# Dummy products on TensorE: 13 instead of 8 at the start of a fused decoder layer, and none near its end

## The chip, the cores and the metric

The kernel runs on one core of one Trainium2 chip. The metric is device time in microseconds (us) of the whole program; the kernel before was timed three times.

## The reference

One decoder layer over 16 sequences of 256 rows of 128 numbers, in three stages, each followed by a residual and a layer norm. The middle stage attends from 256 rows to 64 context rows with 16 heads of 64. The last stage is a gated network whose inputs and weights are rounded in blocks of 16 to the eight magnitudes of FP4.

```python
x = _layernorm(x + _L0_attn_ref(x, Wq, bq, Wk, bk, Wv, bv, Wo, bo, gamma, beta))   # linear attention, 16 heads of 8
x = _layernorm(x + _L0_xattn_ref(x, ctx_1024, Wq, Wk, Wv, Wo))                     # softmax over 64 context rows
x = _layernorm(x + _L0_ffn_ref(x, w_gate, w_up, w_down))
# the last stage:
gate, y = fp4_linear(x, w_gate), fp4_linear(x, w_up)      # 128 -> 352
h = silu(gate) * y
return fp4_linear(h, w_down)                              # 352 -> 128
```

## The kernel before

All weights and the context stay on chip. A sequence is two tiles (t = 0, 1) of 128 rows. The work is written as small steps, one function per step and engine (`gate_up`, `h_transpose`, `down` and so on on TensorE), and every engine has its own list of calls, written out by hand, in which the steps of several sequences b are interleaved. Nothing reorders them at run time: an engine takes its list in order, and each step waits on semaphores for its inputs and for the buffer that it overwrites. So the place of a call in the list sets what can stand behind a wait.

The run has three parts. First comes the set-up, named the fold in the change's description: the cross attention's query and key weights are multiplied into `GT` (`g_product`, written `F<-wqkT` and `TP<-wqkT`), and `GT` with the context into `M` (`m_product`, `F<-ctx_r,GT` and so on, 32 of them, each of three passes over high and low halves of the operands). `project_kv(0)` (`A<-kv_bias_r,ones_r` and `A<-w_attn,xT`) stands between the two `g_product`s. The steady part follows. In the end the last sequence goes tile by tile, with functions whose names begin with `tile_`.

Three calls of `keep_warm` put products on TensorE whose results nobody reads. The first multiplies zeros (`A<-fold`, since the zeros lie in a `fold` buffer) WARM times at the very start. The other two multiply the identity matrix into bank TP0 (`TP<-ident`): 7 times ahead of `h_transpose(13)` and 14 times ahead of `h_transpose(14)`. `h_transpose(b)` transposes `hv`, the rounded activations, which GpSimd finishes at L441 (POOL in the profile); ScalarE (ACT) copies the result to `hT` (L1089), and `down(b)` (L2895) multiplies it with the down weights. In the last sequence `tile_h_transpose` (L2922) and `tile_down` (L2928) do the same for one tile. VectorE (DVE) adds the residual after it (L1915, or L2003 by tile).

An fp32 product shows as two records of the trace in most rows: 8 products of 128x128 are "x16". A transpose of 128x128 is one record.

`xf_r`, two buffers, holds the high and low halves of the transposed inputs of the last stage for sequences 0 to 14; `xfT` is the same in full for the last sequence.

Of the kernel before, what the change touches and what calls it, by code (L numbers as in the profile page):

```python
# [7 lines left out]
FP32R = mybir.dt.float32r  # L8
# [5 lines left out]
P = 128  # L14
# [3 lines left out]
def decoder_layer(nc, x, x_t, attn_w, attn_rows, ctx_t, wq_t, wk_t, wv_t, wo_in, fw_in, out):  # L18
# [40 lines left out]
    with es:  # L59
        def sb(name, shape, dt=FP32):  # L60
            return es.enter_context(nc.sbuf_tensor(name, shape, dt))
# [83 lines left out]
        ssum = several("ssum", 2, [P, HX])  # L145
        srec = several("srec", 2, [P, HX])
# [95 lines left out]
        normed = {"attn": yan_made, "post": x1_made, "cross": x2_made, "ffn": out_made}  # L242

        XO_OF, GU_OF = (A2, A1), ((F0, F1), (S0, S1))

        def part(w, t):
            return w[:, t * P:t * P + P]
# [19 lines left out]
        def wait_free(eng, s, done):  # L267

            if done > 0:
                eng.wait_ge(s, done)  # L270
# [94 lines left out]
        def _(pool):  # L365
# [54 lines left out]
            def fold_halves(b, t):  # L420
                n = T * b + t
                pool.wait_ge(pe_made, n + 1)
                wait_free(pool, ssum_made, n - 1)
                p4 = pe_[n % NPE][:, :].rearrange("p (h s r) -> p h s r", h=HX, s=2)
                ge.tensor_tensor(by_head(fold[n % 2][:, :]), p4[:, :, 0, :], p4[:, :, 1, :], ALU.add).then_inc(fold_made, 1)  # L425

            def probabilities(b, t):
                n = T * b + t
                pool.wait_ge(srec_made, n + 1)
                w = by_head(pe_[n % NPE][:, :])  # L430
                ge.tensor_tensor(w, w, spread(srec[n % 2][:, :], HX, R), ALU.mult).then_inc(pn_made, 1)  # L431

            def x_dequantise(b):
                pool.wait_ge(xg_made, b + 1)
# [507 lines left out]
        def _(act):  # L942
# [101 lines left out]

            def cross_norm(b, t):
                wait_free(act, yf_made, b - 2)
                norm("cross", b, t, x2[b % 3][:, NBX * t:NBX * t + NBX, 0:BLK], blocks(yx[b % 2][:, t, :], NBX))

            def ffn_norm(b, t):
                norm("ffn", b, t, yf[b % 2][:, t, :], yf[b % 2][:, t, :])  # L1050

            def keep_x1T(b):
                act.wait_ge(x1T_made, b + 1)
# [19 lines left out]
                sc.activation(xc, xv[b % 2][:, :], ACT.Abs, scale=STEP).then_inc(xc_made, 1)  # L1073

            def keep_xfT(b):
                act.wait_ge(xf_cut_made, b + 1)
                sc.activation(xf_r[b % 2][:, 0, :], xf_cut[:, :], ACT.Copy).then_inc(xfT_kept, 1)

            def gate_tanh(b, t):
                act.wait_ge(gu_made, T * b + t + 1)  # L1080
# [18 lines left out]
                tile_norm("cross", b, t, x2[b % 3][:, NBX * t:NBX * t + NBX, 0:BLK], blocks(yx[b % 2][:, t, :], NBX))  # L1099

            def tile_ffn_norm(b, t):
                tile_norm("ffn", b, t, yf[b % 2][:, t, :], yf[b % 2][:, t, :])

            def tile_x2_magnitudes(b, t):
                act.wait_ge(xv_made, b + t + 1)
# [1 line left out]

            def tile_keep_xfT(b, t):
                act.wait_ge(xfT_made, b + t + 1)
                sc.activation(part(xfT, t), part(A2, t), ACT.Copy).then_inc(xfT_kept, 1)  # L1110

            def tile_gate_tanh(b, t):
                act.wait_ge(gu_made, T * b + t + 1)
# [558 lines left out]
        def _(dve):  # L1672
# [128 lines left out]
            def statistics(n, b):  # L1801
                y, made = {"attn": (x1[b % NA], ya_made), "post": (x1[b % NA], za_made), "cross": (yx[b % 2], yx_made),
                           "ffn": (yf[b % 2], yf_made)}[n]
                dve.wait_ge(made, b + 1)
# [21 lines left out]
            def score_sums(b, t):  # L1826
                n = T * b + t
                dve.wait_ge(fold_made, n + 1)
                ve.tensor_reduce(ssum[n % 2][:, :], by_head(fold[n % 2][:, :]), AX.X, ALU.add).then_inc(ssum_made, 1)  # L1829

            def score_reciprocals(b, t):
                n = T * b + t
                dve.wait_ge(ssum_made, n + 1)
                wait_free(dve, pn_made, n - 1)
                ve.reciprocal(srec[n % 2][:, :], ssum[n % 2][:, :]).then_inc(srec_made, 1)  # L1835

            def cross_residual(b):
                dve.wait_ge(o_made, T * b + T)
# [85 lines left out]
                ve.tensor_tensor(yx[b % 2][:, t, :], XO_OF[t][:, 0:P], x1[b % NA][:, t, :], ALU.add).then_inc(yx_made, 1)  # L1924

            def tile_statistics(n, b, t):
                y, made = {"cross": (yx[b % 2], yx_made), "ffn": (yf[b % 2], yf_made)}[n]
                dve.wait_ge(made, b + t + 1)
                wait_free(dve, mv_made[n], b)
                ve.bn_stats(stats[n][:, t, :], y[:, t, :]).then_inc(stats_made[n], 1)  # L1930

            def tile_aggregate(n, b, t):
                dve.wait_ge(stats_made[n], b + t + 1)
# [66 lines left out]
            def tile_ffn_residual(b, t):  # L2000
                dve.wait_ge(dn_made, b + t + 1)
                wait_free(dve, out_stored[b % 2], 16 * (b // 2))
                ve.tensor_tensor(blocks(yf[b % 2][:, t, :], NBX), blocks(part(A2, t), NBX), x2[b % 3][:, NBX * t:NBX * t + NBX, 0:BLK],  # L2003
                                 ALU.add).then_inc(yf_made, 1)

            biases()
# [725 lines left out]
        def _(pe):  # L2732
# [121 lines left out]
            def cross_out(b, t):  # L2854
                n = T * b + t
                pe.wait_ge(pT_kept, n + 1)
                if t == 0:
                    pe.wait_ge(vo_kept, b + 1)
                for j in range(NJ):
                    last = te.matmul(A2[:, t * P:t * P + P], pT[n % 2][:, j, :], vo[b % 2][:, j, :], start=(j == 0),  # L2860
                                     stop=(j == NJ - 1))
                last.then_inc(o_made, 1)

            def xf_transpose(b):
# [5 lines left out]
            def gate_up(b, t):  # L2870
                if b == 0 and t == 0:
                    pe.wait_ge(fwT_kept, 4)
                    pe.wait_ge(gu_high_made, 2)
                    pe.wait_ge(gu_low_made, 2)
                pe.wait_ge(xfT_kept, b + 1)
                pe.wait_ge(xf_low_made, b + 1)
# [14 lines left out]
            def down(b):  # L2891
                pe.wait_ge(hT_kept, b + 1)
                for t in range(T):
                    for k in range(NK):
                        last = te.matmul(DN[:, t * P:t * P + P], hT[b % 2][:, t, k * P:k * P + P], w_dn[:, k, :],  # L2895
                                         start=(k == 0), stop=(k == NK - 1))
                last.then_inc(dn_made, 1)

            def tile_cross_out(b, t):
# [12 lines left out]
            def tile_gate_up(b, t):  # L2912
                pe.wait_ge(xfT_kept, b + t + 1)
                for m, bk in enumerate(GU_OF[t]):
                    last = te.matmul(bk[:, 0:I], part(xfT, t), w_gu[:, m, :], start=True, stop=True)
                last.then_inc(gu_made, 1)

            def tile_h_transpose(b, t):
# [5 lines left out]

            def tile_down(b, t):
                pe.wait_ge(hT_kept, b + t + 1)
                for k in range(NK):
                    last = te.matmul(part(A2, t), hT[b % 2][:, t, k * P:k * P + P], w_dn[:, k, :], start=(k == 0), stop=(k == NK - 1))  # L2928
                last.then_inc(dn_made, 1)

            def keep_warm(bank, n, w=ident[:, :]):
# [709 lines left out]
```

## Time and profile before

| | |
|---|---|
| median of 3 runs | 374.0 us (372.37, 374.0, 375.88) |
| profiled execution, its own time | 374.35 us |
| its span, first to last instruction | 372.6 us |
| TensorE busy | 351.0 us, 94% of the span |
| VectorE busy | 307.9 us, 83% |
| GpSimd, ScalarE busy | 269.1 us (72%), 253.4 us (68%) |
| mean granted TensorE clock | 0.996 |

The span is one execution as the hardware profiler saw it; 1.75 us of its own time lie outside of the span. Busy shares are means over parts with different limits, so the parts are read by themselves. The granted clock is 1.0 at 2.4 GHz and 0.5 at 1.2 GHz. PE is TensorE, and DVE, ACT and POOL are the engines named above.

### The profile page before, as it was taken

The numbers are of one execution on the slowest core, as the hardware profiler recorded it, in microseconds if no ns is written. First come the engines' busy times: TensorE is split into PE (matmuls) and PEld (weight loads), VectorE is DVE, ScalarE is ACT, GpSimd is POOL, SyncE is SP. The second block draws the span as 40 slices with busy tenths as digits, with TensorE's granted clock in tenths as the row PEclk, the third lists the DMA queues.
The fourth block names the chain that finished last, engine by engine and source line by source line (L and its number), as shares of the span: only waits on it lengthen the run. The fifth ranks groups of instructions, "written<-read, shape, count | busy, mean of one in ns | idle before, by whom it ended". The sixth has DMA issues, their size and how long they took to land.

```text
span 372.6 us, 7321 instructions
## 1 busy us (share of the span) xinstructions
PE 351.0 (94%) x2143; PEld 268.7 (72%) x2143; DVE 307.9 (83%) x858; ACT 253.4 (68%) x533; POOL 269.1 (72%) x453
## 2 busy tenths in 40 slices
PE   7999998999998999999999999999999999998874
PEld 6688655775775968778678867786777788887663
DVE  2798756658689998869989779979998998999994
ACT  2757867586677678668687767868767656864553
POOL 4403549967988689969779895898989569784535
PEclk9999999999999999999999999999999999999998
DMA  7900100001000001000000000000000000000010
GB/s 251 300 2 16 30 1 14 16 16 29 15 17 14 2 15 43 16 30 17 15 29 14 17 1 17 28 3 0 17 15 2 15 2 0 8 23 14 3 30 28
DMA packets 13586, 10.44 MB, mean 28 GB/s; under 512 B 971, under 2 KB 12396, under 8 KB 13548
## 3 DMA queue, kind: packets, MB, share of 16 engines
q1 hardware_dynamic: 12540, 7.89, 7.0%
q10 hardware_dynamic: 1008, 2.10, 1.7%
q8 instruction: 18, 0.29, 0.3%
q14 instruction: 20, 0.16, 0.1%
HBM read 7.88 MB, written 2.10 MB: 27 GB/s over the span
## 4 chain that ended last, share of the span: by engine, by line
PE 71%; POOL 8%; DVE 8%; issue 6%; ACT 5%; DMA 1%; POOLq 0%; ACTq 0%; DVEq 0%
PE A L2860 13%; PE S L2833 12%; PE TP L2823 7%; PE F L2879 6%; PE TP L2851 6%; PE A L2895 5%; PE A L2784 3%; PE S L2842 3%; PE TP L2762 2%; POOL pe L431 2%; PE S L2762 2%; PE F L2762 2%; PE TP L2888 2%; PE A L2797 2%; DMA wqkT<-in_wk_t 1%
## 5 line engine op out<-in xcount | busy, mean ns | idle before, releaser
L431 POOL TENSOR_TENSOR pe<-pe,srec 128x1024 f32<-128x1024 f32 x32 | 60.9, 1904 | 9.2 <-DVE srec L1835 8.9
L2833 PE MATMUL S<-M,x1T 128*128 128x512 f32 x128 | 60.7, 597 | 1.5 <-ACT pe L1064 1.4
L2860 PEld LDWEIGHTS A<-wvoT,wqkT 128*128 128x128 f32 x480 | 56.4, 192 | 3.1 <-issue 1.8
L2860 PE MATMUL A<-wvoT,wqkT 128*128 128x128 f32 x480 | 58.0, 276 | 0.1
L425 POOL TENSOR_TENSOR fold<-pe 128x512 f32<-128x512 f32 x32 | 40.8, 1276 | 14.5 <-ACT pe L1064 14.2
L1818 DVE TENSOR_REDUCE smax<-S 128x16 fp32r<-128x1024 f32 x32 | 38.7, 1210 | 3.2 <-PE S L2833 3.1
L1064 ACT ACTIVATE pe<-S 128x1024 f32<-128x1024 f32 x32 | 32.6, 1020 | 10.6 <-PE S L2842 10.3
L1069 ACT ACTIVATE wqkT<-TP 128x1024 f32<-128x1024 f32 x32 | 32.6, 1019 | 4.3 <-PE TP L2851 4.1
L2833 PEld LDWEIGHTS S<-M,x1T 128*128 128x128 f32 x128 | 22.2, 190 | 18.3 <-issue 15.3
L2879 PE MATMUL F<-w_gu_r,xf_r 128*128 128x352 f32 x168 | 35.0, 344 | 0.1
L2851 PE MATMUL TP<-ident,pe 128*128 128x128 f32 x256 | 33.5, 274 | 1.6 <-POOL pe L431 1.0
L2851 PEld LDWEIGHTS TP<-ident,pe 128*128 128x128 f32 x256 | 28.8, 140 | 6.2 <-issue 3.1
L2823 PE MATMUL TP<-HW,ctx_f 128*64 128x512 f32 x128 | 31.0, 605 | 0.0
L2879 PEld LDWEIGHTS F<-w_gu_r,xf_r 128*128 128x128 f32 x168 | 26.9, 188 | 4.4 <-issue 3.2
L2895 PEld LDWEIGHTS A<-w_dn,hT 128*128 128x128 f32 x180 | 21.5, 192 | 6.6 <-issue 4.7
L441 POOL TENSOR_TENSOR hv<-hv,ham 128x704 f32<-128x704 f32 x15 | 20.8, 1389 | 6.0 <-DVE hv L1910 5.8
L1829 DVE TENSOR_REDUCE ssum<-fold 128x16 f32<-128x512 f32 x32 | 21.7, 677 | 4.2 <-POOL fold L425 4.2
L416 POOL TENSOR_TENSOR kn<-fk,ky 128x256 f32<-128x256 f32 x16 | 10.1, 632 | 20.7 <-DVE ky L1790 20.6
L2895 PE MATMUL A<-w_dn,hT 128*128 128x128 f32 x180 | 23.0, 277 | 2.0 <-ACT hT L1089 2.0
L2842 PE MATMUL S<-smax,ident_r 128*128 128x512 f32 x64 | 21.8, 422 | 1.7 <-DVE smax L1818 1.7
L409 POOL TENSOR_TENSOR xb<-x_sb,rows 128x512 f32<-128x512 f32 x16 | 20.4, 1275 | 3.9 <-DMA rows<-in_attn_rows 2.7
L1058 ACT ACTIVATE wvoT<-TP 128x1024 f32<-128x1024 f32 x16 | 16.3, 1022 | 6.8 <-PE TP L2823 6.8
(247 smaller groups left out, 890.2 us busy)
## 6 DMA issues: line engine op xcount, KB each, us to landing
xT<-in_x_t SPq DMA_DIRECT2D x16, 128.0 KB, 2.1
x_sb<-in_x SPq DMA_DIRECT2D x16, 128.0 KB, 2.1
out<-yf SPq DMA_DIRECT2D x15, 128.0 KB, 1.8
M<-in_fw SPq DMA_DIRECT2D x1, 560.0 KB, 11.0
wqkT<-in_wq_t ACTq DMA_DIRECT2D x2, 256.0 KB, 4.5
wqkT<-in_wk_t ACTq DMA_DIRECT2D x2, 256.0 KB, 5.8
ctx_f<-in_ctx_t ACTq DMA_DIRECT2D x2, 256.0 KB, 6.9
wvoT<-in_wv_t ACTq DMA_DIRECT2D x1, 512.0 KB, 9.2
```

The lines of the kernel that those rows point to most:

```text
L425: ge.tensor_tensor(by_head(fold[n % 2][:, :]), p4[:, :, 0, :], p4[:, :, 1, :], ALU.add).then_inc(fold_made, 1)
L431: ge.tensor_tensor(w, w, spread(srec[n % 2][:, :], HX, R), ALU.mult).then_inc(pn_made, 1)
L1064: sc.activation(pe_[n % NPE][:, :], S[:, :], ACT.Exp, scale=SCALE).then_inc(pe_made, 1)
L1069: sc.activation(pT[n % 2], TP[:, :].rearrange("p (a n) -> p a n", a=NJ), ACT.Copy).then_inc(pT_kept, 1)
L1818: ve.tensor_reduce(smax[n % 2][:, :], by_head(S[:, :]), AX.X, ALU.max, negate=True).then_inc(smax_made, 1)
L2823: last = te.matmul(TP[par * R:par * R + R, half * BANK:half * BANK + BANK], ctx_f[:, b * R:b * R + R], HW[:, par, 4 * half:4 * half + 4, : ...
L2833: last = te.matmul(S[:, half * BANK:half * BANK + BANK], x1T[b % 2][:, t * P:t * P + P], M[:, b // BH, HC * half:HC * half + HC, b % BH * ...
L2842: last = te.matmul(S[:, half * BANK:half * BANK + BANK], ident_r[:, :], spread(smax[n % 2][:, HC * half:HC * half + HC], HC, R), start=Fal ...
L2851: last = te.transpose(TP[:, j * P:j * P + P], pe_[n % NPE][:, j * P:j * P + P], ident[:, :])
L2860: last = te.matmul(A2[:, t * P:t * P + P], pT[n % 2][:, j, :], vo[b % 2][:, j, :], start=(j == 0), stop=(j == NJ - 1))
L2879: last = te.matmul(bk[:, 0:I], part(xf_r[b % 2][:, left, :], t), w_gu_r[:, right, m, :], start=(n == 0), stop=(n == len(PARTS) - 1))
L2895: last = te.matmul(DN[:, t * P:t * P + P], hT[b % 2][:, t, k * P:k * P + P], w_dn[:, k, :], start=(k == 0), stop=(k == NK - 1))
```

## The change

WARM goes from 8 to 13. Both later calls of `keep_warm` are taken out. `xf_r` is no longer memory of its own: its two buffers become slices of `GT`, which holds the folded weights at the start. `xfT` becomes two buffers, taken in turn by the sequence's number; only the last sequence uses it. The number of `fold`, `ssum` and `srec` buffers gets the name NFO with its old value 2. The diff also brings branches for `WHOLE_GATE`, `SUM_ON_PE` and `TILE_SUM_ON_PE`, which are empty or False, so none of their code is generated; the `down` functions show the pattern.

```diff
-        NXB, NA, NPE = 4, 5, 3
+        NXB, NA, NPE, NFO = 4, 5, 3, 2
...
-        fold = several("fold", 2, [P, HX * R // 2])
+        fold = several("fold", NFO, [P, HX * R // 2])
...
-        xf_r = several("xf_r", 2, [P, 2, T * P], FP32R)
-        xfT = sb("xfT", [P, T * P])
+        xf_r = [GT[:, k, 0:2 * T, :].rearrange("p (s t) n -> p s (t n)", s=2) for k in range(2)]
+        xfT = several("xfT", 2, [P, T * P])
...
+        WHOLE_GATE = ()
+        SUM_ON_PE = ()
+        TILE_SUM_ON_PE = False
...
-        WARM = 8
+        WARM = 13
...
             def tile_down(b, t):
                 pe.wait_ge(hT_kept, b + t + 1)
+                if TILE_SUM_ON_PE:
+                    pe.wait_ge(x2_made, T * b + t + 1)
+                    te.matmul(blocks(part(DN_OF[t], t), NBX), ident[:, :], x2[b % 3][:, NBX * t:NBX * t + NBX, 0:BLK],
+                              start=True, stop=False)
...
             pe.wait_ge(hT_kept, 13)
-            keep_warm(TP0, 7)
             h_transpose(13)
...
             pe.wait_ge(hT_kept, 14)
-            keep_warm(TP0, 14)
             h_transpose(14)
```

On TensorE, at the start of the program: the dummy products of zeros, then `g_product(0)`, `project_kv(0)` and `g_product(1)`. Before:

```order
L2934 MATMUL A<-fold 128x128 x8
L2742 MATMUL F<-wqkT 128x128 x8
L2782 MATMUL A<-kv_bias_r,ones_r 128x256
L2784 MATMUL A<-w_attn,xT 128x256
L2782 MATMUL A<-kv_bias_r,ones_r 128x256
L2784 MATMUL A<-w_attn,xT 128x256
L2742 MATMUL TP<-wqkT 128x128 x8
```

The changed kernel, at the same place (its line numbers are higher throughout, since the file grew):

```order
L2980 MATMUL A<-fold 128x128 x13
L2771 MATMUL F<-wqkT 128x128 x8
L2811 MATMUL A<-kv_bias_r,ones_r 128x256
L2813 MATMUL A<-w_attn,xT 128x256
L2811 MATMUL A<-kv_bias_r,ones_r 128x256
L2813 MATMUL A<-w_attn,xT 128x256
L2771 MATMUL TP<-wqkT 128x128 x8
```

Five more products stand ahead of the first `g_product`; nothing else moved. On TensorE, near the end of the program, from `gate_up(14, 1)` to the last `tile_down`. Before:

```order
L2879 MATMUL F<-w_gu_r,xf_r 128x352 x6
L2934 MATMUL TP<-ident 128x128 x7
L2888 MATMUL TP<-ident,hv 128x128 x6
L2910 MATMUL A<-ident,xv 128x128
L2915 MATMUL F<-w_gu,xfT 128x352 x2
L2895 MATMUL A<-w_dn,hT 128x128 x6
L2910 MATMUL A<-ident,xv 128x128
L2915 MATMUL S<-w_gu,xfT 128x352 x2
L2934 MATMUL TP<-ident 128x128 x14
L2888 MATMUL TP<-ident,hv 128x128 x6
L2895 MATMUL A<-w_dn,hT 128x128 x6
L2922 MATMUL TP<-ident,hv 128x128 x6
```

The changed kernel at the same place:

```order
L2916 MATMUL F<-w_gu_r,GT 128x352 x6
L2925 MATMUL TP<-ident,hv 128x128 x6
L2951 MATMUL A<-ident,xv 128x128
L2956 MATMUL F<-w_gu,xfT 128x352 x2
L2936 MATMUL A<-w_dn,hT 128x128 x6
L2951 MATMUL A<-ident,xv 128x128
L2956 MATMUL S<-w_gu,xfT 128x352 x2
L2925 MATMUL TP<-ident,hv 128x128 x6
L2936 MATMUL A<-w_dn,hT 128x128 x6
L2963 MATMUL TP<-ident,hv 128x128 x6
```

The two rows of `TP<-ident` are gone, and `gate_up` reads its inputs from slices of `GT`. The lists of the other engines hold the same operations and waits in the same order.

## Rows read from the trace of the kernel before

**Rows 1.** The page: TensorE's busy time, and its granted clock in 40 slices

```profile
PE 351.0 (94%) x2143; PEld 268.7 (72%) x2143; DVE 307.9 (83%) x858; ACT 253.4 (68%) x533; POOL 269.1 (72%) x453
...
PEclk9999999999999999999999999999999999999998
```

**Rows 2.** The page: the chain that ended last, by engine

```profile
PE 71%; POOL 8%; DVE 8%; issue 6%; ACT 5%; DMA 1%; POOLq 0%; ACTq 0%; DVEq 0%
```

**Rows 3.** Timeline of TensorE, start; columns: start us, us, operation, records

```profile
1.45 3.78 PE L2934 MATMUL A<-fold 128*128 128x128 f32 x16 [1.45 <-POOL fold L371]
6.57 2.08 PE L2742 MATMUL F<-wqkT 64*128 64x128 f32 x16 [1.34 <-DMA wqkT<-in_wk_t]
...
11.00 1.16 PE L2742 MATMUL TP<-wqkT 64*128 64x128 f32 x16
```

**Rows 4.** Chain that ended last, in order of time, start of the run

```profile
8.65 0.51 PE A L2782
...
10.23 0.86 PE A L2784 x2
...
11.11 0.47 ACT fk L993
...
14.88 0.38 PE A L2782
...
15.82 0.43 PE A L2784 x2
```

**Rows 5.** Timeline: last read of `GT`; by tile: writes of `xf_r`, first and last start

```profile
43.27 0.95 PE L2762 MATMUL F<-ctx_r,GT 128*128 128x512 f32 x3
...
L1876 DVE TENSOR_TENSOR xf_r<-A,xf_cut x15: 390/418/426, 103.3 to 343.0; 128x256 fp32r<-128x256 f32 x15
```

**Rows 6.** Timeline of TensorE, end of the run

```profile
347.79 1.21 PE L2879 MATMUL F<-w_gu_r,xf_r 128*128 128x352 f32 x6
348.85 1.73 PE L2934 MATMUL TP<-ident 128*128 128x128 f32 x14
350.82 0.87 PE L2888 MATMUL TP<-ident,hv 128*128 128x128 f32 x6 [0.25 <-POOL hv L441]
...
352.41 1.42 PE L2915 MATMUL F<-w_gu,xfT 128*128 128x352 f32 x4 [0.46 <-ACT xfT L1110]
353.67 1.50 PE L2895 MATMUL A<-w_dn,hT 128*128 128x128 f32 x12
...
356.62 1.42 PE L2915 MATMUL S<-w_gu,xfT 128*128 128x352 f32 x4 [0.46 <-ACT xfT L1110]
357.88 3.29 PE L2934 MATMUL TP<-ident 128*128 128x128 f32 x28
361.26 0.88 PE L2888 MATMUL TP<-ident,hv 128*128 128x128 f32 x6
363.12 1.58 PE L2895 MATMUL A<-w_dn,hT 128*128 128x128 f32 x12 [0.99 <-ACT hT L1089]
364.54 0.49 PE L2922 MATMUL TP<-ident,hv 128*128 128x128 f32 x3
365.47 0.52 PE L2922 MATMUL TP<-ident,hv 128*128 128x128 f32 x3 [0.44 <-POOL hv L508]
...
367.04 0.94 PE L2928 MATMUL A<-w_dn,hT 128*128 128x128 f32 x6 [0.38 <-DVE yf L2003]
```

**Rows 7.** Timeline of GpSimd, end of the run: the last two `hv` of whole sequences

```profile
349.38 1.39 POOL L441 TENSOR_TENSOR hv<-hv,ham 128x704 f32<-128x704 f32 x1 [0.44 <-DVE hv L1910]
...
359.81 1.39 POOL L441 TENSOR_TENSOR hv<-hv,ham 128x704 f32<-128x704 f32 x1 [0.30 <-DVE hv L1910]
```

**Rows 8.** Busy time of TensorE in short stretches: length, busy, granted clock

```profile
369.00:369.25 0.25, 0.00 (x0) 1.00 0.28 86
...
369.50:370.00 0.50, 0.00 (x0) 0.50 0.17 45
```

**Rows 9.** Timeline of TensorE: a long gap in mid-run

```profile
56.73 1.98 PE L2833 MATMUL S<-M,x1T 128*128 128x512 f32 x4 [1.11 <-ACT pe L1064]
```

More of the change, by code:

```diff
@@ L143, in decoder_layer @@
         smax = several("smax", 2, [P, HX], FP32R)
-        fold = several("fold", 2, [P, HX * R // 2])
-        ssum = several("ssum", 2, [P, HX])
-        srec = several("srec", 2, [P, HX])
+        fold = several("fold", NFO, [P, HX * R // 2])
+        ssum = several("ssum", NFO, [P, HX])
+        srec = several("srec", NFO, [P, HX])
         yx = several("yx", 2, [P, T, P])
@@ L244, in decoder_layer @@
         XO_OF, GU_OF = (A2, A1), ((F0, F1), (S0, S1))
+        DN_OF = (A2, A1) if TILE_SUM_ON_PE else (A2, A2)
+        NSUM = len(SUM_ON_PE)
         def part(w, t):
@@ L422, in fold_halves @@
                 pool.wait_ge(pe_made, n + 1)
-                wait_free(pool, ssum_made, n - 1)
+                wait_free(pool, ssum_made, n - NFO + 1)
                 p4 = pe_[n % NPE][:, :].rearrange("p (h s r) -> p h s r", h=HX, s=2)
-                ge.tensor_tensor(by_head(fold[n % 2][:, :]), p4[:, :, 0, :], p4[:, :, 1, :], ALU.add).then_inc(fold_made, 1)
+                ge.tensor_tensor(by_head(fold[n % NFO][:, :]), p4[:, :, 0, :], p4[:, :, 1, :], ALU.add).then_inc(fold_made, 1)
             def probabilities(b, t):
@@ L1046, in cross_norm @@
                 wait_free(act, yf_made, b - 2)
-                norm("cross", b, t, x2[b % 3][:, NBX * t:NBX * t + NBX, 0:BLK], blocks(yx[b % 2][:, t, :], NBX))
+                y = part(A2, t) if b in SUM_ON_PE else yx[b % 2][:, t, :]
+                norm("cross", b, t, x2[b % 3][:, NBX * t:NBX * t + NBX, 0:BLK], blocks(y, NBX))
             def ffn_norm(b, t):
-                norm("ffn", b, t, yf[b % 2][:, t, :], yf[b % 2][:, t, :])
+                if b in SUM_ON_PE:
+                    wait_free(act, out_stored[b % 2], 16 * (b // 2))
+                norm("ffn", b, t, yf[b % 2][:, t, :], part(DN, t) if b in SUM_ON_PE else yf[b % 2][:, t, :])
             def keep_x1T(b):
@@ L1075, in keep_xfT @@
             def keep_xfT(b):
-                act.wait_ge(xf_cut_made, b + 1)
-                sc.activation(xf_r[b % 2][:, 0, :], xf_cut[:, :], ACT.Copy).then_inc(xfT_kept, 1)
+                if b in WHOLE_GATE:
+                    act.wait_ge(xfT_made, b + 1)
+                    sc.activation(xfT[b % 2][:, :], A2[:, 0:T * P], ACT.Copy).then_inc(xfT_kept, 1)
+                else:
+                    act.wait_ge(xf_cut_made, b + 1)
+                    sc.activation(xf_r[b % 2][:, 0, :], xf_cut[:, :], ACT.Copy).then_inc(xfT_kept, 1)
             def gate_tanh(b, t):
@@ L1101, in tile_ffn_norm @@
             def tile_ffn_norm(b, t):
-                tile_norm("ffn", b, t, yf[b % 2][:, t, :], yf[b % 2][:, t, :])
+                if TILE_SUM_ON_PE:
+                    wait_free(act, out_stored[b % 2], 16 * (b // 2))
+                tile_norm("ffn", b, t, yf[b % 2][:, t, :], part(DN_OF[t], t) if TILE_SUM_ON_PE else yf[b % 2][:, t, :])
             def tile_x2_magnitudes(b, t):
@@ L1109, in tile_keep_xfT @@
                 act.wait_ge(xfT_made, b + t + 1)
-                sc.activation(part(xfT, t), part(A2, t), ACT.Copy).then_inc(xfT_kept, 1)
+                sc.activation(part(xfT[b % 2], t), part(A2, t), ACT.Copy).then_inc(xfT_kept, 1)
             def tile_gate_tanh(b, t):
@@ L1803, in statistics @@
                            "ffn": (yf[b % 2], yf_made)}[n]
-                dve.wait_ge(made, b + 1)
+                if b in SUM_ON_PE and n == "cross":
+                    y = tiles(A2[:, 0:T * P])
+                    dve.wait_ge(o_made, T * b + T)
+                elif b in SUM_ON_PE and n == "ffn":
+                    y = tiles(DN[:, 0:T * P])
+                    dve.wait_ge(dn_made, b + 1)
+                else:
+                    dve.wait_ge(made, b + 1)
                 wait_free(dve, mv_made[n], b)
@@ L1828, in score_sums @@
                 dve.wait_ge(fold_made, n + 1)
-                ve.tensor_reduce(ssum[n % 2][:, :], by_head(fold[n % 2][:, :]), AX.X, ALU.add).then_inc(ssum_made, 1)
+                ve.tensor_reduce(ssum[n % NFO][:, :], by_head(fold[n % NFO][:, :]), AX.X, ALU.add).then_inc(ssum_made, 1)
             def score_reciprocals(b, t):
@@ L1926, in tile_statistics @@
             def tile_statistics(n, b, t):
-                y, made = {"cross": (yx[b % 2], yx_made), "ffn": (yf[b % 2], yf_made)}[n]
-                dve.wait_ge(made, b + t + 1)
+                if n == "ffn" and TILE_SUM_ON_PE:
+                    y = part(DN_OF[t], t)
+                    dve.wait_ge(dn_made, b + t + 1)
+                else:
+                    y, made = {"cross": (yx[b % 2][:, t, :], yx_made), "ffn": (yf[b % 2][:, t, :], yf_made)}[n]
+                    dve.wait_ge(made, b + t + 1 - NSUM)
                 wait_free(dve, mv_made[n], b)
-                ve.bn_stats(stats[n][:, t, :], y[:, t, :]).then_inc(stats_made[n], 1)
+                ve.bn_stats(stats[n][:, t, :], y).then_inc(stats_made[n], 1)
             def tile_aggregate(n, b, t):
@@ L2002, in tile_ffn_residual @@
                 wait_free(dve, out_stored[b % 2], 16 * (b // 2))
-                ve.tensor_tensor(blocks(yf[b % 2][:, t, :], NBX), blocks(part(A2, t), NBX), x2[b % 3][:, NBX * t:NBX * t + NBX, 0:BLK],
+                ve.tensor_tensor(blocks(yf[b % 2][:, t, :], NBX), blocks(part(DN_OF[t], t), NBX), x2[b % 3][:, NBX * t:NBX * t + NBX, 0:BLK],
                                  ALU.add).then_inc(yf_made, 1)
@@ L2858, in cross_out @@
                     pe.wait_ge(vo_kept, b + 1)
+                if b in SUM_ON_PE:
+                    pe.wait_ge(x1_made, T * b + T)
+                    te.matmul(part(A2, t), ident[:, :], x1[b % NA][:, t, :], start=True, stop=False)
                 for j in range(NJ):
-                    last = te.matmul(A2[:, t * P:t * P + P], pT[n % 2][:, j, :], vo[b % 2][:, j, :], start=(j == 0),
-                                     stop=(j == NJ - 1))
+                    last = te.matmul(part(A2, t), pT[n % 2][:, j, :], vo[b % 2][:, j, :],
+                                     start=(j == 0 and b not in SUM_ON_PE), stop=(j == NJ - 1))
                 last.then_inc(o_made, 1)
@@ L2875, in gate_up @@
                 pe.wait_ge(xfT_kept, b + 1)
+                if b in WHOLE_GATE:
+                    for m, bk in enumerate(ffn_banks(b)):
+                        last = te.matmul(bk[:, 0:I], part(xfT[b % 2], t), w_gu[:, m, :], start=True, stop=True)
+                    last.then_inc(gu_made, 1)
+                    return
                 pe.wait_ge(xf_low_made, b + 1)
@@ L2893, in down @@
                 for t in range(T):
+                    if b in SUM_ON_PE:
+                        pe.wait_ge(x2_made, T * b + T)
+                        te.matmul(blocks(part(DN, t), NBX), ident[:, :], x2[b % 3][:, NBX * t:NBX * t + NBX, 0:BLK],
+                                  start=True, stop=False)
                     for k in range(NK):
-                        last = te.matmul(DN[:, t * P:t * P + P], hT[b % 2][:, t, k * P:k * P + P], w_dn[:, k, :],
-                                         start=(k == 0), stop=(k == NK - 1))
+                        last = te.matmul(part(DN, t), hT[b % 2][:, t, k * P:k * P + P], w_dn[:, k, :],
+                                         start=(k == 0 and b not in SUM_ON_PE), stop=(k == NK - 1))
                 last.then_inc(dn_made, 1)
@@ L2914, in tile_gate_up @@
                 for m, bk in enumerate(GU_OF[t]):
-                    last = te.matmul(bk[:, 0:I], part(xfT, t), w_gu[:, m, :], start=True, stop=True)
+                    last = te.matmul(bk[:, 0:I], part(xfT[b % 2], t), w_gu[:, m, :], start=True, stop=True)
                 last.then_inc(gu_made, 1)
@@ L2926, in tile_down @@
                 pe.wait_ge(hT_kept, b + t + 1)
+                if TILE_SUM_ON_PE:
+                    pe.wait_ge(x2_made, T * b + t + 1)
+                    te.matmul(blocks(part(DN_OF[t], t), NBX), ident[:, :], x2[b % 3][:, NBX * t:NBX * t + NBX, 0:BLK],
+                              start=True, stop=False)
                 for k in range(NK):
-                    last = te.matmul(part(A2, t), hT[b % 2][:, t, k * P:k * P + P], w_dn[:, k, :], start=(k == 0), stop=(k == NK - 1))
+                    last = te.matmul(part(DN_OF[t], t), hT[b % 2][:, t, k * P:k * P + P], w_dn[:, k, :],
+                                     start=(k == 0 and not TILE_SUM_ON_PE), stop=(k == NK - 1))
                 last.then_inc(dn_made, 1)
```

6 lines of the change are left out of this document (3 added, 3 removed).

## Prediction

> **What bounds the kernel now.** I read the page first. TensorE is busy for 94% of the span [rows 1], and the chain that ended last lies on it for 71% [rows 2]. For most of the run TensorE is the bound: whatever moves TensorE at the start moves the end by as much. The page's row of the granted clock reads full everywhere but in its last slice [rows 1]. Here the reader has to be careful, since the durations say something else of the start. Sixteen records of `F<-wqkT` take 2.08 us at 6.57, and the same sixteen of `TP<-wqkT` 1.16 us at 11.00 [rows 3]. The dummy products of zeros take 3.78 / 8 = 0.47 us each, and the dummy products of the identity late in the run 3.29 / 14 = 0.235 us [rows 3, 6]. That is the factor of two between 1.2 and 2.4 GHz. So TensorE starts at the lower level, whatever the row says, and rises between 10.2 us and 11.0 us, some way into the stretch that begins at 6.57 and has no gap; the 8 dummy products ahead of it did not bring the rise, and a gap of 1.34 us, in which TensorE waits for the load of a weight, parts the two [rows 3].
>
> The second view is the chain of waits in order of time. From 6.57 to 11.09 it lies on TensorE, at the lower level, then passes to ScalarE's `fk`, which reads `project_kv(0)` [rows 4], and from about 15 us it lies on TensorE again. So what is saved ahead of 11.09 goes through.
>
> The third is the end. There TensorE is not the bound. `h_transpose(13)` starts at 350.82, right behind GpSimd's `hv`, which ends at 349.38 + 1.39 = 350.77; `h_transpose(14)` starts at 361.26, behind the next `hv`, which ends at 359.81 + 1.39 = 361.20 [rows 6, 7]. The dummy products end before either, at 350.58 and 361.17. They stand in time in which TensorE would wait anyway.
>
> **The change, part by part.**
>
> *Five more products of zeros.* If the clock stays low, 13 products take 13 x 0.47 = 6.14 us and end at 1.45 + 6.14 = 7.59, which is 1.02 us after `g_product(0)` could start [rows 3]. What they may give is an earlier rise, because TensorE now has no gap from 1.45 on. I bound it from both sides. (a) The rise comes as the eighth product ends, at 5.23: the other five take 5 x 0.235 = 1.2 us and end at 6.4, ahead of the load. `g_product(0)` then takes 1.16 for 2.08, so 0.92 less, and `project_kv(0)`, which took from 8.65 to 11.09 = 2.44 us, takes what `project_kv(1)` takes at the upper level, 14.88 to 16.25 = 1.37 us, so 1.07 less [rows 3, 4]. Sum -2.0. (b) The rise comes as the thirteenth ends, at 7.59: 1.02 late, 0.92 and 1.07 less, sum -1.0. (c) It comes no earlier than before, at 11: +1.0. Nothing in the trace speaks for (c), since the stretch from 6.57 got its rise while `g_product` and `project_kv` ran and that stretch is shorter than the new one. I take the middle of (a) and (b), **-1.5 us**. Behind it VectorE's and ScalarE's operations up to 14.9 keep their durations, and the products that follow are at the upper level either way, so the sum stays -1.5 to the end part of the run.
>
> The moment of the rise need not be the same in each execution. The Trainium skill (TensorE: Matmul & The Clock Gate, Part 1) says that the same kernel runs another number of slow products from run to run. No row here shows that; three times from 372.37 to 375.88 us would bear it.
>
> *No dummy products at the end, directly.* 7 x 0.235 = 1.7 us and 3.29 us of TensorE go, and what is late next is `hv` at 350.77 and 361.20, so the starts of both `h_transpose`s stay, within 0.06 us. **0 us**. Their cover, in the other sense, is gone: they were what kept TensorE running. Without them it stands still from 349.00 to 350.82 (1.8 us) and from 358.04 to 361.26 (3.2 us) [rows 6].
>
> *What the gaps do to the clock.* The longest gaps of TensorE that the trace shows between the rise and the last product are 1.1 us, such as the one ahead of 56.73 [rows 9], and the clock stayed up through them. The only fall is at the end: the last product ends at 367.98, the granted clock is still 1.0 at 369.25 and 0.5 at 369.5 [rows 6, 8]. So 1.3 to 1.5 us of standing still, after a stretch broken by two short waits, was enough there. A gap of 3.2 us after one that has waits on both sides is far on the side of the fall, and one of 1.8 us is in between.
>
> The Trainium skill (same page, the section on HAM oscillation) ties the fall to idle gaps that outlast the gate's idle test, and its examples are gaps of several us while waiting for loads. Read strictly it would let both of these gaps pass, and the time would be that of rival 1. The fall in rows 8 came sooner than that reading allows, so I give it a chance but not the forecast.
>
> *What the lower level costs at the end.* A record of 128 columns costs 0.236 us at the start and 3.29 / 28 = 0.118 at the end, so the lower level adds 0.118 per record [rows 3, 6]. After the second gap stand `h_transpose(14)` with 6 records (+0.71), `down(14)` with 12 (+1.42), two tile transposes with 3 each (+0.35 each) and two `tile_down`s with 6 each (+0.71 each), together +4.25 [rows 6]. All are on the path: `h_transpose(14)` starts as `hv` lands; ScalarE's copy and `down(14)` wait for it; the tile transposes stand behind `down(14)` in TensorE's list; each `tile_down` is waited for by VectorE's residual, and the second waits for that too. What hides some of it is the wait of 0.44 us between the two transposes [rows 6], which goes. Upper bound +3.8. Lower bound: the fall comes only after `h_transpose(14)`, and the clock is back for the last `tile_down`, since `down(14)` and what follows now run without a gap: 3.8 - 0.71 - 0.71 = +2.4. I take the middle, **+3.1 us**.
>
> After the first gap, if the clock falls there: `h_transpose(13)` +0.71, the transpose behind it +0.12, `tile_gate_up(15, 0)` with 4 records of 352 columns +4 x 0.118 x 352 / 128 = +1.30, `down(13)` +1.42 [rows 6], in all +3.5; VectorE is busy nearly without a break there and waits for `down(13)` at its residual, so nearly all would count. Slowed so, TensorE has hardly a gap and should rise before `down(13)` ends, as it did at the start; I put the cost given a fall at +1.7, half, and the fall at one half, so **+0.8 us**, with 0 and +3.5 as ends.
>
> *The buffers.* `GT` is last read at about 44 us and `xf_r` first written at 103.3 [rows 5], so the slices bring no new wait, and none is in the lists. `xfT` has one user; a second buffer releases nothing. **0 us**.
>
> **Sum.** -1.5 + 0 + 0.8 + 3.1 + 0 = +2.4. On the profiled execution's own 374.35 us (span 372.6 and 1.75 around it) this is 376.75; the median of the runs is 0.35 lower, so the forecast is **376.4 us**, 0.6% slower.
>
> **The rivals.**
>
> 1. *The clock holds through both gaps.* Then only the start counts: 374.0 - 1.5 = 372.5 us. For it: the fillers were in time that TensorE does not need. Against it: the fall 1.3 to 1.5 us after the last product [rows 8]. Chance 0.20.
>
> 2. *The clock falls in the first gap and stays down through `down(13)`.* Then the later part of the first term is paid in full, on VectorE's path, and the second gap on top: -1.5 + 3.0 + 3.8 = +5.3, with the start's smaller gain +5.8: 379.3 to 379.8 us, slower by over 1%. It decides from the point where the lower level lasts beyond `tile_gate_up(15, 0)`. For it: 1.8 us is longer than the pause before the one fall that the trace has; against it: the first gap has busy TensorE before it, and the slowed products fill the waits behind it. With half of that cost, 378 us, it is just as much over the mark. Chance 0.25 for 377.7 and above by this way.
>
> 3. *The products of zeros only push the fold.* The clock rises at 11 as before, `g_product(0)` starts at 7.59, +1.0 in place of -1.5: 378.9 us. Chance 0.05.
>
> That the change does not do what it says has no case of its own: the lists show the products gone and added.
>
> **How the numbers follow.** The forecast has a chance of 0.50 with its own range from 375.0 (-1.5 - 0 + 2.4, rounded) to 377.7; rival 1 has 0.20, rival 2 0.25, rival 3 0.05. The range for 8 in 10 reaches from rival 1 with its larger gain at the start (374.0 - 2.0) = 372.0 to the middle of rival 2, 379.6. One per cent, 3.7 us, is about what a measurement of this kernel can tell from no change. Slower by over 1% is above 377.7: rivals 2 and 3, 0.30, less what of rival 2 ends just under, plus what of the forecast ends over: 0.30. Faster by over 1%, below 370.3, has no mechanism here: 0.04 is left for it. Within 1%: 0.66.
>
> **What the changed profile would show.** The 26 records of `A<-fold` take less than 6.1 us and the last ones about 0.118 each; `F<-wqkT` takes some 1.2 us and ScalarE's `fk` starts near 9.6. Late in the run the granted clock is 0.5 from within or just after the gap between `tile_gate_up(15, 1)` and `h_transpose(14)`, `down(14)` takes about 3 us for 1.58, and the wait of `h_transpose(14)` for `hv` is over 3 us long. The forecast is wrong if the clock reads 1.0 through that gap, or if `hv` comes earlier without the dummy products, as neither VectorE nor GpSimd depends on them.

## The result and the profile after

The changed kernel took 376.25 us (median of 6 runs, 375.44 to 376.7), the kernel before 373.76 us (6 runs, 372.37 to 375.88). The ratio is 1.0075, with a 95% interval from 1.0053 to 1.0097: by it the change costs 0.75%, and the medians lie 2.5 us apart. The profiled execution took 376.27 us, with a span of 374.5 us, so 1.77 us lie outside of the span, as before.

The page of the changed kernel, first the busy times, then the granted clock in 40 slices:

```profile
PE 349.2 (93%) x2111; PEld 266.9 (71%) x2111; DVE 307.8 (82%) x858; ACT 253.2 (68%) x533; POOL 268.6 (72%) x453
...
PEclk9999999999999999999999999999999999999878
```

TensorE is busy for 1.8 us less than before [rows 1] and the run is longer. The clock's row is now below full in its last three slices, where before it was in the last alone.

The timeline of TensorE at the start of the changed kernel:

```profile
1.45 5.00 PE L2980 MATMUL A<-fold 128*128 128x128 f32 x26 [1.45 <-POOL fold L380]
6.38 1.16 PE L2771 MATMUL F<-wqkT 64*128 64x128 f32 x16
...
9.69 1.16 PE L2771 MATMUL TP<-wqkT 64*128 64x128 f32 x16 [0.76 <-DMA wqkT<-in_wk_t]
...
13.07 0.39 PE L2811 MATMUL A<-kv_bias_r,ones_r 128*128 128x256 f32 x1 [0.22 <-DVE fq L1789]
```

The 13 products of zeros take 5.00 us, not the 6.14 that the lower level would need: the clock rose while they ran. The first `g_product` then takes 1.16 us for 2.08 [rows 3], and `project_kv(1)` starts at 13.07 for 14.88 [rows 4], 1.81 us earlier. A wait is new: the second `g_product` stands 0.76 us for the second half of `wk_t`. The chain that ended last shows it too. It lay on TensorE from 6.57 us before, and now it lies on that load until 9.64:

```profile
2.68 6.96 DMA wqkT<-in_wk_t
```

The timeline of TensorE at the end of the changed kernel:

```profile
349.20 0.85 PE L2925 MATMUL TP<-ident,hv 128*128 128x128 f32 x6 [1.89 <-POOL hv L450]
349.95 0.35 PE L2951 MATMUL A<-ident,xv 128*128 128x128 f32 x1
350.76 2.69 PE L2956 MATMUL F<-w_gu,xfT 128*128 128x352 f32 x4 [0.46 <-ACT xfT L1128]
353.24 1.62 PE L2936 MATMUL A<-w_dn,hT 128*128 128x128 f32 x12
355.45 0.33 PE L2951 MATMUL A<-ident,xv 128*128 128x128 f32 x1 [0.58 <-DVE yf L1940]
356.24 1.42 PE L2956 MATMUL S<-w_gu,xfT 128*128 128x352 f32 x4 [0.46 <-ACT xfT L1128]
360.96 1.51 PE L2925 MATMUL TP<-ident,hv 128*128 128x128 f32 x6 [3.31 <-POOL hv L450]
363.47 2.90 PE L2936 MATMUL A<-w_dn,hT 128*128 128x128 f32 x12 [0.99 <-ACT hT L1105]
366.16 1.30 PE L2963 MATMUL TP<-ident,hv 128*128 128x128 f32 x6
367.68 0.91 PE L2973 MATMUL A<-w_dn,hT 128*128 128x128 f32 x6 [0.22 <-ACT hT L1140]
368.97 0.94 PE L2973 MATMUL A<-w_dn,hT 128*128 128x128 f32 x6 [0.38 <-DVE yf L2032]
```

Follow the difference to the kernel before from row to row [rows 6]. `h_transpose(13)` starts 1.62 us earlier: the gain of the start has come through 330 us nearly whole. Behind the gap of 1.89 us `tile_gate_up(15, 0)` takes 2.69 us for 1.42. At its counterpart for the other tile, 356.24 for 356.62, 0.38 us of the gain are left. Behind the gap of 3.31 us `down(14)` takes 2.90 us for 1.58, and the last product starts at 368.97 for 367.04, 1.93 us late. So the first gap cost 1.24 us and the second 2.31 us in this execution, and the span is 1.9 us longer.

The granted clock of the changed kernel in short stretches, for TensorE (stretch, its length, busy time and records, clock):

```profile
350.00:351.00 1.00, 0.54 (x3) 0.54 0.03 8
351.00:352.00 1.00, 1.00 (x2) 0.50 0.00 0
352.00:353.00 1.00, 1.00 (x3) 0.50 0.00 0
353.00:354.00 1.00, 1.00 (x7) 0.76 0.00 0
354.00:355.00 1.00, 0.87 (x8) 1.00 0.00 0
...
359.50:360.00 0.50, 0.00 (x0) 1.00 0.00 0
360.00:362.00 2.00, 1.04 (x5) 0.58 0.22 66
362.00:364.00 2.00, 1.01 (x5) 0.50 0.00 0
364.00:366.00 2.00, 2.00 (x12) 0.50 0.00 0
366.00:368.00 2.00, 1.78 (x11) 0.72 0.00 0
368.00:370.00 2.00, 1.52 (x12) 1.00 0.00 0
```

The clock falls at about 350.1, after the first gap has ended, and is back in mid-353. It falls again at about 360.3, inside the second gap, and is back at about 367. The slow rows of the timeline lie in exactly these stretches.

GpSimd's `hv`, for which the second `h_transpose` waits, in the changed kernel's timeline:

```profile
359.43 1.39 POOL L450 TENSOR_TENSOR hv<-hv,ham 128x704 f32<-128x704 f32 x1 [0.31 <-DVE hv L1935]
```

It is 0.38 us earlier than before [rows 7], as much as is left of the gain. It takes as long as before, so the dummy products had not delayed it.

### The profile page after: what moved, and what is told of

The parts are those of the page before. It is cut to its first block, busy times and chain, and to the rows that moved or that the text cites. A ratio compares the mean times of both kernels' runs of the same rounds, so it can differ in the third digit from the quotient of the medians.

```text
span 374.5 us, 7259 instructions
## 1 busy us (share of the span) xinstructions
PE 349.2 (93%) x2111; PEld 266.9 (71%) x2111; DVE 307.8 (82%) x858; ACT 253.2 (68%) x533; POOL 268.6 (72%) x453
## 4 chain that ended last, share of the span: by engine, by line
PE 70%; POOL 8%; DVE 7%; issue 7%; ACT 5%; DMA 2%; ACTq 0%; POOLq 0%; DVEq 0%
PE A L2892 13%; PE S L2862 12%; PE TP L2852 7%; PE F L2916 6%; PE TP L2880 6%; PE A L2936 5%; PE S L2871 3%; PE A L2813 2%; POOL pe L440 2%; PE TP L2791 2%; DMA wqkT<-in_wk_t 2%; PE F L2791 2%; PE S L2791 2%; PE TP L2925 2%; PE A L2826 2%
## 5 line engine op out<-in xcount | busy, mean ns | idle before, releaser
L2916 PE MATMUL F<-w_gu_r,GT 128*128 128x352 f32 x168 | 35.2, 344 | 0.1
L2916 PEld LDWEIGHTS F<-w_gu_r,GT 128*128 128x128 f32 x168 | 27.0, 189 | 4.4 <-issue 3.2
L2936 PEld LDWEIGHTS A<-w_dn,hT 128*128 128x128 f32 x180 | 23.0, 202 | 7.0 <-issue 5.4
L2936 PE MATMUL A<-w_dn,hT 128*128 128x128 f32 x180 | 24.4, 288 | 2.0 <-ACT hT L1105 2.0
```

Source lines behind the costliest of these rows:

```text
L2936: last = te.matmul(part(DN, t), hT[b % 2][:, t, k * P:k * P + P], w_dn[:, k, :], start=(k == 0 and b not in SUM_ON_PE), stop=(k == NK - 1))
```

## The experiments

All kernels were timed in five rounds beside the kernel before. The medians of the kernel before in the three groups of experiments were 373.94, 373.90 and 373.54 us. The ratios are the recorded ones, not quotients of these medians. Each edit is shown against the changed kernel.

**Both late groups put back** (of the change, the products of zeros and the moved buffers are left):

```diff
             pe.wait_ge(hT_kept, 13)
+            keep_warm(TP0, 7)
             h_transpose(13)
...
             pe.wait_ge(hT_kept, 14)
+            keep_warm(TP0, 14)
             h_transpose(14)
```

> The changed kernel with both late groups of dummy products put back (7 and 14), so that of the change only the five more products of zeros and the moved buffers are left. Theory (the start gives, the gaps cost): no fall of the granted clock before the last product, the gain at the start (1.8 us at the second project_kv in the trace) comes through to the end, 372.0 us, ratio to the kernel before 0.995 to 0.996. Rival (the start's gain is used up in mid-run by other waits, and the end alone explains the loss): no difference from before, ratio 1.000.

Measured: 372.62 us (372.32 to 373.18, 12 runs), ratio 0.9969 (0.9957 to 0.9981). The gain at the start lasts, and is 1.3 us in the median. It is less than the expectation had, which took it from one trace; the kernel with one product of zeros, below, shows why. This kernel is faster than both the kernel before and the changed one. Its timeline of TensorE at the end:

```profile
356.11 3.29 PE L2980 MATMUL TP<-ident 128*128 128x128 f32 x28
359.49 0.87 PE L2925 MATMUL TP<-ident,hv 128*128 128x128 f32 x6
361.36 1.58 PE L2936 MATMUL A<-w_dn,hT 128*128 128x128 f32 x12 [0.99 <-ACT hT L1105]
...
365.27 0.94 PE L2973 MATMUL A<-w_dn,hT 128*128 128x128 f32 x6 [0.39 <-DVE yf L2032]
```

The durations are those of before [rows 6] and everything is 1.8 us earlier.

**Eight products of zeros again, no late ones:**

```diff
-        WARM = 13
+        WARM = 8
```

> The changed kernel with 8 products of zeros again and no late dummy products. Theory: the clock falls in both gaps as in the changed kernel, and the gain at the start is missing: 1.2 + 2.3 = 3.5 us above the kernel before, with up to 2 us more or less by where the falls come, 377.3 us, ratio 1.008 to 1.013. Rival (the products of zeros give nothing that lasts): the same as the changed kernel, 376.2 us, ratio 1.0065 to 1.0075.

Measured: 378.0 us (376.56 to 378.27, 6 runs), ratio 1.0117 (1.0097 to 1.0138). That is 4.1 us over the kernel before, so the removal alone costs more than the 3.5 us taken from one trace, and the products of zeros are worth 1.7 us here. The rival is out. The profiled execution, at 376.56 us the fastest of the six by 1.0 us, has an early rise with only 8 products:

```profile
1.45 3.78 PE L2980 MATMUL A<-fold 128*128 128x128 f32 x16 [1.45 <-POOL fold L380]
6.39 1.16 PE L2771 MATMUL F<-wqkT 64*128 64x128 f32 x16 [1.16 <-DMA wqkT<-in_wk_t]
```

All eight products are slow and the first real one is fast, though TensorE stood still for 1.16 us in between.

**Only the 14 put back:**

```diff
             pe.wait_ge(hT_kept, 14)
+            keep_warm(TP0, 14)
             h_transpose(14)
```

> The changed kernel with the 14 dummy products ahead of h_transpose(14) put back, not the 7. Theory: the fall in the first gap stays (it cost 1.2 us in the one execution looked at, and may not come in every one), the one in the second does not come: 376.2 - 2.3 = 373.9 us, ratio 0.998 to 1.001. Rival (the second gap costs all of it): 372.1 us, ratio 0.995 to 0.996, like the kernel with both groups.

Measured: 373.92 us (373.27 to 375.23, 12 runs), ratio 1.0014 (1.0 to 1.0029). Against the kernel with both groups the open first gap costs 1.3 us. In the profiled execution, one of the two fastest, there was no slow row behind the gap of 1.91 us. The mean clock was 0.997 in these two and 0.992 to 0.995 in the other ten. None of the ten was profiled; the lower means say that the clock fell in them.

**Only the 7 put back:**

```diff
             pe.wait_ge(hT_kept, 13)
+            keep_warm(TP0, 7)
             h_transpose(13)
```

> The changed kernel with the 7 dummy products ahead of h_transpose(13) put back, not the 14. Theory: no fall in the first gap, a fall in the second in each execution: 372.1 + 2.3 to 3.8 = 374.4 to 375.9 us, ratio 1.002 to 1.006. Rival (both gaps must be open for a fall, since the 3.2 us of the second are not enough by themselves): no fall, 372.1 us, ratio 0.995 to 0.996.

Measured: 376.51 us (374.66 to 376.62, 6 runs), ratio 1.0066 (1.0042 to 1.0089), 3.9 us over the kernel with both groups, 0.6 us above the expected range. The rival is out: the second gap is enough by itself. Its timeline of TensorE:

```profile
359.80 1.51 PE L2925 MATMUL TP<-ident,hv 128*128 128x128 f32 x6 [3.30 <-POOL hv L450]
362.31 2.90 PE L2936 MATMUL A<-w_dn,hT 128*128 128x128 f32 x12 [0.99 <-ACT hT L1105]
365.00 1.49 PE L2963 MATMUL TP<-ident,hv 128*128 128x128 f32 x6
366.52 1.62 PE L2973 MATMUL A<-w_dn,hT 128*128 128x128 f32 x6
368.52 0.94 PE L2973 MATMUL A<-w_dn,hT 128*128 128x128 f32 x6 [0.38 <-DVE yf L2032]
```

All products behind the gap but those of the last `tile_down` are at the lower level here. The clock in short stretches shows the lower level from about 358.1 to 368.4 us:

```profile
358.00:358.50 0.50, 0.00 (x0) 0.64 0.00 0
...
368.00:368.50 0.50, 0.14 (x1) 0.62 0.00 0
```

The two costs, 1.3 and 3.9 us, are together more than the changed kernel's 3.6 us over the kernel with both groups. The last experiments come back to that.

**The buffers on their own again,** with 13 products of zeros and both groups:

```diff
-        xf_r = [GT[:, k, 0:2 * T, :].rearrange("p (s t) n -> p s (t n)", s=2) for k in range(2)]
+        xf_r = several("xf_r", 2, [P, 2, T * P], FP32R)
```

> 13 products of zeros, both late groups of dummy products, and xf_r as two buffers of its own again: the kernel with both groups put back, less the move into GT. Theory (the move costs nothing): 372.6 us as that kernel, ratio 0.9969, within 0.0015. Rival (the place of the buffers costs or gives something in the 30 gate_up steps): another time than that kernel's 372.6 by over 0.6 us.

Measured: 372.72 us (372.42 to 373.07, 12 runs), ratio 0.9978 (0.9962 to 0.9994), for 372.62 with the slices. The move costs nothing that can be measured.

**Dummy transposes for the late dummy products:**

```diff
+            def keep_turning(bank, n):
+                for _ in range(n):
+                    te.transpose(bank[:, 0:P], ident[:, :], ident[:, :])
...
+            keep_turning(TP0, 14)
             h_transpose(13)
...
+            keep_turning(TP0, 28)
             h_transpose(14)
```

> 13 products of zeros; the late dummy products are replaced by dummy transposes of the identity that fill the same time (14 for the 7, 28 for the 14, one record of 0.118 us each). Theory of the gaps (any work of TensorE keeps the clock up): 372.6 us, ratio 0.997, no fall before the last product. Rival (the rule of the Trainium skill that a transpose does not count as busy): the clock falls as with no dummies, and the time is the changed kernel's, 376.3 us, ratio 1.0075 by this or more, since dummies that run at the lower level also end later (28 x 0.236 = 6.6 us from 356.1, past hv).

Measured: 372.85 us (372.47 to 373.25, 12 runs), ratio 0.9974 (0.9959 to 0.9989). Its timeline of TensorE in the second gap:

```profile
356.51 3.22 PE L2979 MATMUL TP<-ident 128*128 128x128 f32 x28
359.89 0.88 PE L2925 MATMUL TP<-ident,hv 128*128 128x128 f32 x6 [0.16 <-POOL hv L450]
361.76 1.58 PE L2936 MATMUL A<-w_dn,hT 128*128 128x128 f32 x12 [0.99 <-ACT hT L1105]
```

Transposes keep the clock up as well as products do. The Trainium skill (TensorE: Matmul & The Clock Gate, Part 4) says that a transpose does not count as busy in the same way; these fp32 transposes kept the clock up here, with full speed behind them in the rows above, and the measurement decides. Whether transposes alone would bring the rise, no run shows.

**Half-filled gaps,** 3 dummy products for 7 and 7 for 14:

```diff
+            keep_warm(TP0, 3)
             h_transpose(13)
...
+            keep_warm(TP0, 7)
             h_transpose(14)
```

> 13 products of zeros; 3 late dummy products for 7 and 7 for 14, so that each gap is about half filled (0.7 of 1.8 us and 1.65 of 3.2 us, right behind the work before it). Idle rests of about 1.1 and 1.6 us are left. Theory (what counts is how much of TensorE's time is idle there): the first gap, now no longer than the gaps of mid-run, holds; the second is near the edge, so that executions part into two groups: 372.6 for some and about 375 for others, median between 372.6 and 375. Rival (a gap has to be closed fully): 376 us or more, ratio 1.006 or more.

Measured: 374.48 us (12 runs, 374.36 without the longest), ratio 1.0016 (0.9996 to 1.0036). Its times are three from 372.57 to 373.01, eight from 374.2 to 374.86, and one of 509.21 (below). The two groups came as expected, but not where. Its timeline of TensorE:

```profile
349.15 0.87 PE L2925 MATMUL TP<-ident,hv 128*128 128x128 f32 x6 [1.14 <-POOL hv L450]
...
350.75 2.26 PE L2956 MATMUL F<-w_gu,xfT 128*128 128x352 f32 x4 [0.46 <-ACT xfT L1128]
352.81 2.36 PE L2936 MATMUL A<-w_dn,hT 128*128 128x128 f32 x12
...
361.10 0.87 PE L2925 MATMUL TP<-ident,hv 128*128 128x128 f32 x6 [1.65 <-POOL hv L450]
362.97 1.58 PE L2936 MATMUL A<-w_dn,hT 128*128 128x128 f32 x12 [0.99 <-ACT hT L1105]
```

It is the first gap, at 1.14 us and with a wait of 0.46 us next to it, behind which the clock fell, at about 351.2. Behind the second, 1.65 us, it held in this execution. The gaps of 1.1 us in mid-run hold [rows 9]. So the length of one gap does not decide alone. That the waits around it count too fits these rows but is not shown, and chance has a part: the same kernel took under 373.1 us in three executions, at a mean clock of 0.999 to 1.0.

**One product of zeros** for 13, with both late groups:

```diff
-        WARM = 13
+        WARM = 1
```

> 1 product of zeros for 13; both late groups are in. Theory (the kernel before falls into two groups of times, about 372.4 and 374.0, by whether its 8 products of zeros and the fold behind them bring the rise early; with one product they never do): all executions near 374.1 to 374.5 us, none at 372.4, ratio 1.001 to 1.003. Rival (the groups of the kernel before come from elsewhere): two groups again, 372.4 among them.

Measured: 374.37 us (373.85 to 374.76, 12 runs), ratio 1.0022 (1.0003 to 1.004). No time is near 372.4. The kernel before, in the 35 runs beside it, had 12 times from 372.01 to 372.72 and 23 from 373.63 to 374.94, and none between. With 13 products of zeros and both groups, all 12 are at or under 373.18. Read from the times, 8 products of zeros bring the early rise in about one execution of three, 13 in each that was timed, and one in none. Two traces fit the reading: the profile of the kernel before, at 374.35 us, has the late rise, and that of the kernel with 8 products of zeros and none late, the fastest of its six, has the early one. The timeline of TensorE with one product of zeros has the first `g_product` at the lower level:

```profile
1.45 0.80 PE L2980 MATMUL A<-fold 128*128 128x128 f32 x2 [1.45 <-POOL fold L380]
6.90 2.08 PE L2771 MATMUL F<-wqkT 64*128 64x128 f32 x16 [4.65 <-DMA wqkT<-in_wk_t]
```

**Twenty products of zeros,** with both late groups:

```diff
-        WARM = 13
+        WARM = 20
```

> 20 products of zeros; both late groups are in. With a rise at 4.9 to 7.5 us, as in the traces so far, the products of zeros end at 1.45 + 20 x 0.235 plus half of the slow stretch, 7.9 to 9.1 us, so g_product(0) starts 1.2 to 2.3 us later than with 13. Theory (what the start gives is bounded by the second load of wk_t, which lands near 9.6 us, so part of the delay is hidden): fk and the fold 0.8 to 1.5 us later than with 13, 373.3 to 374.1 us, ratio 0.998 to 1.001. Rival (from 13 on the number is free, since the load hides it all): 372.6 us, ratio 0.997.

Measured: 374.48 us (373.4 to 374.89, 12 runs), ratio 1.0024 (1.0006 to 1.0042). Its timeline of TensorE:

```profile
1.45 7.06 PE L2980 MATMUL A<-fold 128*128 128x128 f32 x40 [1.45 <-POOL fold L380]
8.44 1.16 PE L2771 MATMUL F<-wqkT 64*128 64x128 f32 x16
...
10.83 1.16 PE L2771 MATMUL TP<-wqkT 64*128 64x128 f32 x16
```

The fold starts at 8.44 and there is no wait for the load any more. All of the delay beyond 13 counts, 1.9 us, somewhat more than I expected. So more is not better: of the numbers tried, 1, 8, 13 and 20, the best is 13, which brings the rise and ends about as the load lands. What lies between them was not tried.

**The changed kernel and the one with only the 7, side by side,** both as above.

> The changed kernel itself, timed beside the next one on the same chip: 376.2 us, ratio 1.0065 to 1.0075. If the costs of the two gaps add (1.3 for the first, 3.9 for the second, from the kernels with one group each against the one with both), it is 1.3 us above the next kernel; if the fall in the first gap shortens the slow stretch behind the second, as the two traces have it (6.8 us at the lower level for 10.2), both have the same time.

> The kernel with the 7 dummy products and without the 14, again, beside the changed kernel. If the costs add: 375.0 us, 1.3 us under the changed kernel. If the slow stretch is shortened by a first fall: 376.3 us, the same as the changed kernel, with the clock's slow stretch longer here than there in the traces.

Measured: the changed kernel 376.3 us (375.39 to 376.68), ratio 1.0064 (1.0039 to 1.0089); with the 7, 375.94 us (375.37 to 376.59), ratio 1.0061 (1.0037 to 1.0085). Over both times that they ran, 12 runs each, the medians are 376.26 and 376.13: the same. By the sum of the single costs the changed kernel should be 1.3 us longer, and it is not.

The spans say where the difference lies. Medians of the spans: 370.85 us with both groups, 372.05 with only the 14, 373.5 with only the 7 (12 executions), 374.5 for the changed kernel (12). So within the span the first gap costs 1.2 us, the second 2.65, and both 3.65: there the costs do add, within the scatter. What does not add lies outside of the span. It is 1.72 to 1.81 us in the changed kernel's executions and 1.73 to 1.82 in those with both groups, but 1.94 to 3.39 in all 12 with only the 7. The traces of this kernel show one more difference. A packet of 0.02 MB on a queue that the profile calls the instructions' moves after the last instruction, at about 375.9 us in the first trace (span 374.1) and 375.1 in the second (span 373.3). In the first:

```profile
q8 instruction: 1, 0.02, 1.5%
```

The profile of the half-filled kernel has such a packet as well, at about 373.5 with a span of 372.4, and its executions have up to 2.36 us outside of the span; no other profile has one so late. So of the 3.5 us by which the 12 runs with only the 7 are slower than the kernel with both groups, about 0.9 lies where no slowed product stands. That the packet is what takes this time is argued from the two coming together, not shown; no run moved it.

The slow stretch behind the second gap is not what parts the two kernels either. With the 7 it was from 358.1 to 368.4 in the first trace, but from 360.3 to 367.1 in the second, as long as in the changed kernel (360.3 to 367.1). Each of these is one execution, and how the moments of fall are set stays open.

## Why the prediction was right

*The start.* Forecast -1.5 us between -2.0 and +1.0; measured -1.3 us in the medians (372.62 for 373.94). The rise does come while the products of zeros run, as (a) and (b) had it, and rival 3, at 378.9 us, came in no profile and no time of the changed kernel. Two things were missing from the working. The kernel before gets the early rise by luck in a third of its executions, so the gain over its median is smaller than over the profiled one, which was of the slower kind. The working took from the one trace that 8 products do not bring the rise. And in the changed kernel the second `g_product` waits for the second half of `wk_t`, which the working left out. `fk` starts 2.15 us earlier (8.96 for 11.11), but `project_kv(1)` only 1.81. Where 13 products of zeros stand first, that `g_product` starts between 9.30 and 10.20 us, and its wait for the load is from nothing to 1.00 us.

*No direct gain at the end.* Forecast 0, since `hv` ends behind the dummy products. `hv` comes no earlier than the gain at the start brings it, and TensorE waits 1.89 and 3.31 us for it. Right.

*The falls.* A fall in or behind the second gap came in every profile of a kernel with that gap open, the latest 1.5 us after its end (8 products of zeros, none late). Rival 1, which goes by the strict reading of the Trainium skill's section on HAM oscillation (TensorE: Matmul & The Clock Gate), would have given 372.5 us; the kernels with both groups show what that would look like. That section draws its falls from waits of several us. This case's traces do not agree: here 1.9 us with short waits around it came before a fall in three profiles of four, and once 1.14.

*The sizes.* Forecast +0.8 for the first gap and +3.1 for the second, together +3.9; measured together +3.6 (376.26 for 372.62) to +4.1 (8 products of zeros, no late ones, for the kernel before). By the spans the first gap costs 1.2 us and the second 2.65. So the first term was too small and the second somewhat too large, and the sum is nearer than its terms. In the first, two errors work against each other: the chance of a fall was put at one half and was about ten in twelve, and its cost at 1.7 us and was about 1.2. In the second, the middle of the bounds has half of the first `tile_down` and half of `h_transpose(14)` slow. The changed kernel's trace has the first `tile_down` at 0.91 us for 0.83, so at the upper level, and lost 2.31 us in all, just under the lower bound of 2.4. The times of the kernel with only the 7, 3.5 us over the kernel with both groups in 12 runs, hold time outside of the span, which the forecast had no term for. Its price of a record at the lower level holds: `down(14)` takes 2.90 us where 1.58 + 1.42 = 3.00 was worked out. Rival 2 needed the lower level through `down(13)`. The profile of the kernel with 8 products of zeros and none late has it (slow from 349.9 to 356.7), and the first gap cost 2.45 us there, but the fall behind the second came late and cost only 1.4. The changed kernel's times, up to 376.7, did not reach rival 2's 377.7.

*The buffers.* Forecast 0; measured 0.1 us, within the noise.

So the mechanism was right in all its parts, and the forecast of 376.4 us for 376.25 is closer than its working: that the terms' errors cancel to 0.15 us is luck.

## What to carry to other kernels

Work that an engine does while it waits costs nothing on the timeline and can still hold something up: before dummy products are taken out of a gap in TensorE's work, look at what runs behind the gap, and price it at half the clock. Dummy products at the start paid here when they ran without a break into the real work; the best of the numbers tried ends about as the first weights land. Where a kernel's times fall into two groups, ask which of its stages has a moment that is set by chance, before a difference of one group's size is explained. And before costs are said not to add, compare the spans as well as the times: here the part that did not add lay outside of the span.

## What was not expected of the hardware

The granted clock in the page reads full before its first change, though the products of the first microseconds run at half of the later speed: 0.47 us for a product that takes 0.235 us later. The rise came while only zeros were multiplied.

The clock fell behind a gap of 1.14 us once, 2.0 us after its end, and held through one of 1.65 us in the same execution. It fell at 350.1 in the changed kernel, when the gap of 1.89 us had already been over for 0.9 us. With 8 products of zeros, the rise came in or before a gap of 1.16 us in which TensorE did nothing.

One execution of the half-filled kernel took 509.21 us, with a mean granted clock of 0.657; it has no profile, and no other of the runs came near it. With a clock of 0.5 or 1.0 that is the lower level for more than two thirds of the run.
